# Down-projection bias in a fused attention and MoE kernel: from products on TensorE to an add on VectorE, with the gate on ScalarE

## What is computed

```
x = x + attention(layernorm(x), ctx, ...)
xf = layernorm(x).reshape(-1, 256)
logits = xf @ Wr + br
topk_val, topk_idx = top_k(logits, 2)
scores = softmax(topk_val)
h = einsum('nd,edh->enh', xf, W1) + b1[:, None, :]      # h is 1024 wide
a, g = split(h, 2)
act = silu(a) * g
out_e = einsum('enh,ehd->end', act, W2) + b2[:, None, :]
out = sum over the 2 chosen experts of out_e * score
x = x + out
```

## Time and profile before

| | |
|---|---|
| three runs | 1325.05, 1326.02, 1320.41 us; median 1325.05 |
| profiled execution | 1321.74 us, its span 1319.8 us |
| busy over the span | TensorE 89%, VectorE 78%, ScalarE 57%, GpSimd 47% |
| mean granted TensorE clock | 0.961 of full speed |
| TensorE clock and share of the DMA engines from 700 to 1250 us | 1.00; 0.70 |
| HBM traffic | 125.17 MB read, 47.60 MB written |

### The profile page before, as it was taken

How to read it: one execution, slowest core, us unless ns; L and a number is a source line. 1 busy time by engine, 2 the same in 40 slices (tenths; PEclk the granted TensorE clock), 3 DMA queues, 4 the chain that set the end, 5 groups by cost and what they waited for, 6 DMA issues and landing times.

```text
span 1319.8 us, 38223 instructions
## 1 busy us (share of the span) xinstructions
PE 1177.9 (89%) x12680; PEld 1044.8 (79%) x12681; DVE 1032.4 (78%) x2933; ACT 757.1 (57%) x1497; POOL 625.0 (47%) x729
## 2 busy tenths in 40 slices
PE   4999999999999999840499999999999999999986
PEld 3677777677777777530499999999999999999886
DVE  4788999999999988844478888888788887887763
ACT  4676666666666666422365555555655556555542
POOL 5245666666666665553034444344343443432323
PEclk9999999999999999955699999999999999999998
DMA  4122333333332322216667776767767677675653
GB/s 162 36 75 84 98 99 96 97 100 101 100 94 92 97 72 74 76 63 204 213 177 165 183 163 178 183 161 182 170 171 187 163 180 172 166 188 145 157 137 36
DMA packets 106958, 174.78 MB, mean 132 GB/s; under 512 B 13600, under 2 KB 82400, under 8 KB 106848
## 3 DMA queue, kind: packets, MB, share of 16 engines
q1 hardware_dynamic: 77808, 134.45, 32.0%
q0 software_dynamic: 26592, 36.46, 16.6%
q10 hardware_dynamic: 2448, 2.44, 0.6%
HBM read 125.17 MB, written 47.60 MB: 131 GB/s over the span
## 4 chain that ended last, share of the span: by engine, by line
PE 41%; DMA 8%; issue 2%; POOL 1%; SPq 1%; DVE 0%; ACTq 0%; ACT 0%; POOLq 0%; DVEq 0%
PE bank L1065 8%; PE bank L1066 8%; PE bank L1067 8%; DMA out_rows<-y_gated,block_tokens 6%; PE bank L1080 4%; PE bank L1081 4%; PE bank L1082 4%; PE bank L1054 2%; DMA w_raw<-in_L_ffn_W 1%; PE bank L1083 1%; POOL out_rows L1313 1%; SPq L1014 0%; DMA routed_rows<-block_rows 0%; DVE act L1268 0%; ACTq L988 0%
## 5 line engine op out<-in xcount | busy, mean ns | idle before, releaser
L1313 POOL DMA_INDIRECT out_rows<-y_gated,block_tokens x142 | 267.1, 1881 | 438.0 <-DVE y_gated L1283 340.6
L1065 PE MATMUL bank<-block_T_hi,w_hi 128*128 128x256 f32 x1136 | 332.0, 292 | 11.7 <-DVE block_T_lo L1258 11.7
L1066 PE MATMUL bank<-block_T_lo,w_hi 128*128 128x256 f32 x1136 | 319.8, 282 | 0.0
L1067 PE MATMUL bank<-block_T_hi,w_lo 128*128 128x256 f32 x1136 | 319.6, 281 | 0.0
L1065 PEld LDWEIGHTS bank<-block_T_hi,w_hi 128*128 128x128 f32 x1136 | 217.2, 191 | 13.6 <-DVE block_T_lo L1258 9.6
L1066 PEld LDWEIGHTS bank<-block_T_lo,w_hi 128*128 128x128 f32 x1136 | 216.9, 191 | 0.0
L1067 PEld LDWEIGHTS bank<-block_T_hi,w_lo 128*128 128x128 f32 x1136 | 216.1, 190 | 0.0
L1151 ACT ACTIVATE act_hi<-act 128x512 fp32r<-128x512 f32 x142 | 89.8, 632 | 196.1 <-DVE act L1268 196.1
L492 ACT ACTIVATE probs_T<-bank 128x512 f32<-128x512 f32 x256 | 132.1, 603 | 97.5 <-PE bank L321 97.5
L1268 DVE SCALAR_TENSOR_TENSOR act<-bank,block_b,silu_a 128x256 f32<-128x256 f32 x284 | 124.3, 479 | 68.2 <-PE bank L1067 60.8
L1241 DVE TENSOR_TENSOR w_lo<-w_raw,w_hi 128x1024 fp32r<-128x1024 f32 x142 | 167.9, 1223 | 11.8 <-ACT w_hi L1128 11.4
(11 more groups left out here) (159 smaller groups left out, 2501.0 us busy)
## 6 DMA issues: line engine op xcount, KB each, us to landing
w_raw<-in_L_ffn_W SPq DMA_DIRECT2D x71, 1024.0 KB, 6.3
block_rows<-routed_rows SPq DMA_DIRECT2D x71, 272.0 KB, 3.3
x_in<-in_x SPq DMA_DIRECT2D x64, 128.0 KB, 2.3
ctx_T<-in_ctx SPq DMA_DIRECT2D x16, 512.0 KB, 3.6
x_res<-in_x SPq DMA_DIRECT2D x64, 128.0 KB, 2.7
out_rows<-x SPq DMA_DIRECT2D x64, 128.0 KB, 2.2
w_raw<-in_L_ffn_W SPq DMA_DIRECT2D x8, 512.0 KB, 7.7
out_rows<-y_gated,block_tokens POOLq DMA_INDIRECT x142, 4.3
```

What stands on the lines that cost most here:

```text
L1065: mm(dst, w1h[:, k, c, at:at + P], xh[:, k, c, :], start=(c == 0), stop=False)
L1066: mm(dst, w1h[:, k, c, at:at + P], xl[:, k, c, :], start=False, stop=False)
L1067: last = mm(dst, w1l[:, k, c, at:at + P], xh[:, k, c, :], start=False, stop=(c == KC - 1))
L1313: nc.gpsimd.indirect_dma_start(out=out[:, :], out_offset=bass.IndirectOffsetOnAxis(ap=tk[:, u % U, t:t + 1], axis=0), in_=yg[:, u % 2, t, ...
```

## The change

For each block SP also loads the expert's row of b2 into all 128 partitions (a buffer of four; before the fifth it waits until the bias of the block four back has been added). VectorE reads the down products from PSUM, adds that row and writes the sum to `y_gated`; ScalarE then multiplies it in place by the gate, and GpSimd's adds wait for ScalarE. The bias products, their split into parts, the memsets and the small DMAs that placed them are gone. ScalarE's `gate(u - 2)` stands in slot u between the high part of the first half of act and the silu of the second half.

```diff
@@ experts: tiles and semaphores
-        bp = sb("bias_parts", [P, E * D], BF16)
-        bsp = sb("bias_split", [P, E * D // P], F32)
-        bpt = sb("bias_part_tiles", [P, 3, E * D // P], BF16)
-        sel3 = sb("three_ones", [P, P], BF16)
+        b2r = sb("block_b2_rows", [P, U, D], F32)
...
+        s_b2 = [sem(f"block_b2_loaded{k}") for k in range(U)]; s_yb = sem("bias_added"); s_b2f = sem("b2_buffer_free")
@@ SP: load_w1, first
                 sp.dma_start(w1r[:, u % 2], w1.rearrange("e k n -> (e k) n")[bass.ds(e * D, D), :]
                              .rearrange("(c p) n -> p c n", p=P)).then_inc(s_w1[u % 2], 16)
+                if real(i, u - U):
+                    sp.wait_ge(s_yb, n(i, u - U, ET))
+                    sp.sem_inc(s_b2f, 1)
+                sp.dma_start(b2r[:, u % U, :], b2[bass.ds(e, 1), :].to_broadcast([P, D])).then_inc(s_b2[u % U], 16)
...
-                sp.dma_start(bsp[:], b2.rearrange("e n -> (e n)").rearrange("(p n) -> p n", p=P)).then_inc(s_bl, 16)
...
-                sp.wait_ge(s_bs, 5)
-                sp.wait_ge(s_bz, 1)
-                for k in range(3):
-                    sp.dma_start(bp[k:k + 1, :].rearrange("o (p n) -> o p n", p=P), bpt[:, k, :]).then_inc(s_bd, 16)
@@ TensorE: down
                     if real(i, u - 1):
-                        pe.wait_ge(s_yg, n(i, u - 1, ET, t + 1))
+                        pe.wait_ge(s_yb, n(i, u - 1, ET, t + 1))
...
-                        mm(dst, l, w2h[:, bass.ds(at, D)], start=False, stop=False)
-                    mm(dst, sel3[:], bp[:, bass.ds(e * D, D)], start=False, stop=True).then_inc(s_y, 1)
+                        last = mm(dst, l, w2h[:, bass.ds(at, D)], start=False, stop=(c == FC - 1))
+                    last.then_inc(s_y, 1)
@@ ScalarE
+            def gate(i, u):
+                for t in range(ET):
+                    act.wait_ge(s_yb, n(i, u, ET, t + 1))
+                    nc.scalar.activation(yg[:, u % 2, t, :], yg[:, u % 2, t, :], ACT.Copy,
+                                         scale=gt[:, u % U, t:t + 1]).then_inc(s_yg, 1)
...
                 act_hi(i, u, 0)
+                if real(i, u - 2):
+                    gate(i, u - 2)
                 silu(i, u, 1)
...
-            turns(act, first, slot, lambda i, u: None)
+            def last(i, u):
+                gate(i, u - 2)
+                gate(i, u - 1)
+
+            turns(act, first, slot, last)
@@ VectorE
-            V.memset(sel3[:], 0.0).then_inc(s_t, 1)
...
-            bstep(V.tensor_copy(bpt[:, 0, :], bsp[:]))
-            bstep(V.tensor_tensor(bsp[:], bsp[:], bpt[:, 0, :], ALU.subtract))
...
-            def gate(i, u):
-                dve.wait_ge(s_meta, n(i, u))
+            def bias(i, u):
+                dve.wait_ge(s_b2[u % U], n4(i, u))
                 if real(i, u - 2):
                     dve.wait_ge(s_add, n(i, u - 2, 16 * ET))
                 for t in range(ET):
                     dve.wait_ge(s_y, n(i, u, ET, t + 1))
-                    V.tensor_scalar(yg[:, u % 2, t, :], bank[6 + t][:, 0:D], gt[:, u % U, t:t + 1], None,
-                                    ALU.mult).then_inc(s_yg, 1)
+                    V.tensor_tensor(yg[:, u % 2, t, :], bank[6 + t][:, 0:D], b2r[:, u % U, :], ALU.add).then_inc(s_yb, 1)
@@ GpSimd
-            nc.gpsimd.memset(bp[:].bitcast(U32), 0).then_inc(s_bz, 1)
```

More of the change, by code:

```diff
@@ L945, in experts @@
         s_cnt = sem("counts_summed"); s_t = sem("table_step"); s_tab = sem("tables_done")
-        s_bl = sem("biases_loaded"); s_bs = sem("bias_step"); s_bd = sem("bias_parts_placed"); s_bz = sem("bias_zeroed")
+        s_b2 = [sem(f"block_b2_loaded{k}") for k in range(U)]; s_yb = sem("bias_added"); s_b2f = sem("b2_buffer_free")
         s_b1l = sem("b1_rows_loaded"); s_b1t = sem("b1_transposed"); s_b1 = sem("b1_columns_copied")
@@ L983, in n2, with n4 @@
             return i * (U // 2 * 16) + (u // 2 + 1) * 16
+        def n4(i, u):
+            return i * 16 + (u // U + 1) * 16
         def idle_rows(eng, experts):
@@ L1102, in slot @@
                         pe.wait_ge(s_w2l, E)
-                        pe.wait_ge(s_bd, 16 * 3)
                     down(i, u - 1, expert(i, u - 1))
@@ L1167, in _ @@
             V = nc.vector
-            V.memset(sel3[:], 0.0).then_inc(s_t, 1)
             V.memset(pad, 0.0).then_inc(s_t, 1)
-            dve.wait_ge(s_t, 2)
-            V.memset(sel3[0:3, :], 1.0)
-            steps = [2]
+            dve.wait_ge(s_t, 1)
+            steps = [1]
             def step(ins):
@@ L1213, in _ @@
             V.tensor_copy(b1T[:], bank[5][:, 0:E * 2 * FC]).then_inc(s_b1, 1)
[L1214 to L1220, removed]
-            bstep(V.tensor_copy(bpt[:, 0, :], bsp[:]))
-            bstep(V.tensor_tensor(bsp[:], bsp[:], bpt[:, 0, :], ALU.subtract))
-            bstep(V.tensor_copy(bpt[:, 1, :], bsp[:]))
-            bstep(V.tensor_tensor(bsp[:], bsp[:], bpt[:, 1, :], ALU.subtract))
-            bstep(V.tensor_copy(bpt[:, 2, :], bsp[:]))
             def first():
@@ L1297, in slot @@
                 if real(i, u - 1):
-                    gate(i, u - 1)
-            turns(dve, first, slot, lambda i, u: gate(i, u - 1))
+                    bias(i, u - 1)
+            turns(dve, first, slot, lambda i, u: bias(i, u - 1))
         @block.gpsimd
         def _(pool):
-            nc.gpsimd.memset(bp[:].bitcast(U32), 0).then_inc(s_bz, 1)
             def slot(i, u):
```

## The result

The changed kernel takes 1392.0 us (median of 6 runs, 1389.8 to 1393.7) against 1323.7 for the kernel before (median of 6, 1316.7 to 1326.7). The ratio is 1.053 with a 95% interval of 1.050 to 1.055: slower by 68 us. The forecast was 1371 us, range 1340 to 1405. The profiled execution took 1392.97 us, its span 1391.2.

What follows compares the result with a forecast made beforehand. TensorE was taken as the bound until one late pair of adds locks the kernel. Three blocks at 8.90 (-0.7), fifty-five locked (+47.9) and the tail (+2.6) gave +49.8 on 1321.74: 1371 us, range 1340 to 1405.

Steps and rivals of the forecast that it cites:

- The mechanism: GpSimd's adds move beside the weight load, land late, delay token read and next load, and lock the kernel; chance 0.80.
- the locked pace: Block time once late adds and weight loads keep meeting: 10.01 us against 9.14, +47.9 us over fifty-five blocks.
- at nothing: The per-block b2 load on SP's queue, 128 KB behind the weight load, was counted as costing no time.
- my upper bound: The most the b2 loads could cost if each delayed the add: 0.44 us per block, 28 us in all.
- the 3.7 us of the earlier trace: Landing time of a GpSimd add in a free block, started 3.6 us behind a weight load.
- the straight line: Interpolation of add landing times between 6.41 and 3.7 us, giving 5.7 us at 1.5 us behind the weight load.
- the chain's 0.12 per product: Cost of one bias product on TensorE in the chain of waits: 0.12 us, a block 0.24 us.
- that nothing is gained: Rival: TensorE's bias products cost nothing, so removing them gains nothing; called excluded by 0.12 us per product, no chance given.
- the nearest row: The 128x256 SBUF to SBUF operation on ScalarE, 402 ns, taken as the price of one gate.
- The free state: Rival: second adds land under 5.1 us and no early lock; 1307 us, up to 1317 if locking late; chance 0.12.
- the threshold of 5.1 us: Longest landing of the second add that would not delay VectorE's token read; 6.2 us was expected, 1.1 us late.
- The ring of four blocks: Rival: late landings stop TensorE but GpSimd's round isn't longest; 9.15 to 9.4 us per block, 1317 to 1333 us; chance 0.06.

Runs made afterwards that it cites:

- e4: The changed kernel with U = 8 in place of 4: eight buffers and a token read that waits for adds eight blocks back; 1287.7 us, ratio 0.977.
- e5: The kernel of e4 with one number put back: VectorE's token read waits for the adds four blocks back again; 1429.3 us, ratio 1.083.
- e10: The changed kernel with SP's two steps exchanged, so the weight load is issued ahead of the row load; 1304.5 us, ratio 0.987.
- e7: The kernel before with one 128x2560 memset on GpSimd between the two adds of the fourth block; 1369.7 us, ratio 1.038.
- e7b: As e7 on the kernel before, but with a shorter memset of 128x512 at the same place; 1367.3 us, ratio 1.036.
- e9: The changed kernel with b2 loaded for the first four blocks only, so later output bias is wrong; 1382.6 us, ratio 1.047.
- e3: The changed kernel with all experts' b2 loaded once (1 MB) and one more table read per block on VectorE; 1390.1 us, ratio 1.055.
- e2: The kernel before with only the gate moved to ScalarE: bias products kept, no b2 load, VectorE copies the down products; 1379.2 us, ratio 1.044.
- e6: The changed kernel with the gate multiplied by VectorE right behind each bias add, none on ScalarE; 1313.3 us, ratio 0.995.
- e1: The changed kernel with ScalarE's two gates moved ahead of the first silu of the same slot; 1395.7 us, ratio 1.058.
- e11: The changed kernel with the edits of e4 and e10 together: U = 8 and the weight load ahead of the row load; 1300.6 us, ratio 0.984.

## Why the prediction was right, and where not

**The mechanism** held step by step. The adds moved beside the weight load (0.20 and 2.11 us behind it; forecast were 0.3 ahead and 1.5 behind). The second add landed in 5.5 us in the first block and in 7.65 on average once locked (forecast 6.0 to 6.4, then 6.5 to 7.1). The token read waited, the load moved with it, and the third pair was locked. e4, e5 and e10 show that it takes both links: the read that waits for adds four blocks back, and the weight load that waits for the read. Take away either, and the same late gates cost nothing. That a locked kernel stays locked is shown by e7 and e7b.

**The size**: forecast 10.01 us per locked block, measured 10.31; over 63 blocks that is 19 of the 21 us by which 1371 fell short. The term that was too small is the locked pace, taken unchanged from the kernel before. A locked round is the landing of its second add, 0.8 us to the next pair and 1.86 us between the two adds. Only the landing differs between the locked kernels: over pairs 6 to 51 it is 7.60 us on average in the change, and 7.32 and 7.35 in e7 and e7b, where VectorE still does the gate.

The b2 load, which the sum had "at nothing", may be a part of that. Its wait had not "been met": the bias of the block four back is added just behind the weight load's issue (load 908.63, bias adds, b2 load 910.72; timelines of VectorE and SP's queue):

```profile
909.74 0.75 DVE L1277 TENSOR_TENSOR y_gated<-bank,block_b_rows 128x256 f32<-128x256 f32 x2
```

What the load costs isn't settled: 7 to 9.5 us by e9, nothing by e3; my upper bound was 28. Here the Trainium skill, DMA: Bandwidth & Descriptors, section Queues, rings and completion order, had led me to the lower end: by the order within one ring the b2 rows take no turn from the add. e9 speaks against that use of it, and so does e5, in which b2 comes right behind the load and the adds beside it take 8.4 us against 7.65; e3 doesn't. The rest, about 0.15 us per block, is there without b2 loads too: 10.15 in e9, against 9.99 in e7. (e2 has 10.17, but its profiled execution was the slowest of its four, 10 us above their median, and that alone is 0.15 us per block.) What lengthens the landings when the gate is on ScalarE isn't known.

**A reading that was off**: the 3.7 us of the earlier trace rows is the quickest kind of free add. Of the first adds of pairs 3 to 56, 14 land in 3.8 us on average, and 40 in 4.7, those for which GpSimd takes about 2.5 us and not 1.55. From 4.7 the straight line would have given 5.9 us in place of 5.7. It changes no step.

**TensorE's part**: 0.24 us per block was forecast from the chain's 0.12 per product; free blocks gained 0.16 (e6, e10) at U = 4. In the locked state the products gain nothing that can be seen: e2, which keeps them, has 10.17 us per block, and e9, which has neither them nor the b2 loads, 10.15. So "that nothing is gained" can't be excluded by the 0.12 us of the earlier trace rows; that price holds only where TensorE is the bound.

**ScalarE and VectorE**: the gate takes 494 ns, not 402, a pair 0.89 us; the nearest row had no scale from memory. The bias add takes 416 ns. No engine waited for either: in the waits of the change from 700 to 1320 us, VectorE's `act` has no wait for ScalarE's silu, and GpSimd waited for a gate once (7.0 us).

**The rivals.** The free state exists and is worth what it was priced at: 1307 forecast, 1304.5 in e10, up to 1317 with a late lock, 1313 in e6. It wasn't reached, since the threshold of 5.1 us for a landing was missed by 0.4 us in the first pair already. The ring of four blocks did not hold the pace at 9.15 to 9.4 us either: GpSimd's own round was the longer one.

## What to carry to other kernels

An operation that is moved to an idle engine moves everything behind it; ask when its consumer's DMAs then start and which big load they meet. Where a large load is issued only after an event that waits for small DMAs to land, the two can fall into step and stay so: look for one late event after which the pace never recovers, and break the tie at the cheapest place, here the order of two issues on SP, or a ring of eight token buffers in place of four.

## What was not expected of the hardware

- **How wide the bad place is.** Landing time of a 128-row add by its start against the issue of the 1 MB load: 4.2 us at -4 (before, free), 4.5 at -2.1 (change, first adds, mean), 6.1 at -1.66 (e7b, one add), 6.9 at -1.38 (before, one first add), 7.7 at -1.32 (e1, one add), 7.65 at -0.24 (change, mean), 6.1 at +1.5 and 5.0 at +2.5 (e4, means), 3.9 at +4.3 (e10, mean). An add that starts up to about 1.4 us before the load is hit nearly as hard as one that starts with it; at 2.1 us before it isn't.
- **The late add comes at the same pair in each program.** The second add of pair 57 starts 4.7 to 7.2 us behind the first, instead of 1.9 to 2.8, in each program; for instance 1176.88 and 1182.00 in the kernel before, 1168.48 and 1173.59 in e6, 1246.26 and 1251.19 in the change, 1159.15 and 1166.35 in e4, 1173.73 and 1179.18 in e10. The times differ, the count doesn't. GpSimd's program has no more work there; the cause is open.
- **TensorE's step between equal products varies by program** at clock 1.00: blocks take 9.14 us with U = 4 and 9.27 with U = 8 with the bias products, and 8.98 (e10) and 8.74 (e11, up to pair 57) without them. Nothing but buffers, their addresses and the loop's length differs within a pair. No run here says which of them it is.
